# One fused attention-and-experts kernel: other places for its last batch's shared work, for four list scatters and for a semaphore's first count

## The reference

```python
def ffn(x, gate_w, w1, w2, w3, ws1, ws2, ws3):
    scores = softmax(xf @ gate_w.T)
    weights, idx = top_k(scores, 2)                  # 2 of 8 experts per token
    h = einsum('td,eid->eti', xf, w1)
    g = silu(h) * einsum('td,eid->eti', xf, w3)
    eo = einsum('eti,edi->etd', g, w2)
    y = einsum('etd,te->td', eo, comb)               # comb: the two weights
    z = silu(xf @ ws1.T) * (xf @ ws3.T) @ ws2.T      # the shared expert
    return y + z
x = x + tanh(g_xattn) * cross_attention(layernorm(x), ctx)
x = x + tanh(g_ffn) * ffn(layernorm(x))
```

## Time and profile before

| what | us |
|---|---|
| median of 3 runs (lowest, highest) | 464.53 (464.41, 466.38) |
| the profiled execution, its own time | 467.39 |
| its span in the trace | 465.7 |
| TensorE busy | 409.3 (88%) |
| VectorE busy | 306.2 (66%) |
| ScalarE busy | 239.5 (51%) |
| GpSimd busy | 228.1 (49%) |

### The profile page before, as it was taken

The page is one execution under the profiler, slowest core; times in us unless marked ns, Lnnn a source line. Parts: engine busy times, 40 slices in busy tenths (PEclk is TensorE's granted clock), DMA queues, the critical chain, the costliest instruction groups (busy, mean ns, idle before and its releaser), DMA issues.

```text
span 465.7 us, 8278 instructions
## 1 busy us (share of the span) xinstructions
PE 409.3 (88%) x2739; PEld 221.6 (48%) x2740; DVE 306.2 (66%) x663; ACT 239.5 (51%) x432; POOL 228.1 (49%) x205
## 2 busy tenths in 40 slices
PE   1877887999999999898868889989999999999980
PEld 1454443555545554464433345445555555555540
DVE  4977998789588876898839659954444444444430
ACT  2786875676647766756214136834443434344330
POOL 4008434537266762589350212755556565565422
PEclk9988998999999999999979899999999999999996
DMA  8930002606006076176168477966567666566553
GB/s 303 419 104 2 0 1 68 227 2 223 4 1 227 2 288 134 41 262 192 59 59 155 138 272 225 158 116 109 118 98 131 128 100 130 94 132 108 96 67 45
DMA packets 20768, 58.64 MB, mean 126 GB/s; under 512 B 3521, under 2 KB 3777, under 8 KB 20354
## 3 DMA queue, kind: packets, MB, share of 16 engines
q1 hardware_dynamic: 11234, 37.77, 25.9%
q0 software_dynamic: 9504, 20.48, 24.5%
HBM read 35.54 MB, written 22.70 MB: 125 GB/s over the span
## 4 chain that ended last, share of the span: by engine, by line
PE 54%; DVE 17%; POOL 8%; issue 8%; DMA 5%; ACT 5%; POOLq 1%; SPq 0%; DVEq 0%; ACTq 0%
PE bank L1664 40%; PE bank L1669 9%; DVE arena L1057 4%; ACT arena L701 3%; DMA lists<-pair,slot 2%; DVE mv L1093 2%; POOL lists L573 2%; POOL arena L588 2%; PE bank L1817 2%; PE bank L1806 2%; PE bank L1794 2%; POOL GT L613 2%; DVE mx L1178 1%; POOL ln L555 1%; DMA listed<-lists 1%
## 5 line engine op out<-in xcount | busy, mean ns | idle before, releaser
L1664 PE MATMUL bank<-arena,GT 128*128 x468 | 107.4, 379 | 2.8 <-issue 2.8
L685 POOL DMA_INDIRECT out<-rows,entry x39 | 61.8, 1586 | 72.1 <-issue 31.3
L1664 PE MATMUL bank<-arena,gT 128*128 (+1 forms) x336 | 80.2, 376 | 1.4 <-ACT rows L1032 1.0
L1664 PEld LDWEIGHTS bank<-arena,GT 128*128 128x128 f16 x468 | 45.8, 98 | 49.7 <-issue 3.5
L701 ACT ACTIVATE arena<-bank 128x512 f16<-128x512 f32 (+1 forms) x88 | 48.7, 587 | 26.1 <-PE bank L1664 12.0
L662 POOL DMA_INDIRECT rows<-xrows,entry x39 | 38.9, 997 | 43.4 <-DVE entry L1455 18.2
L1057 DVE SCALAR_TENSOR_TENSOR arena<-bank,arena 128x512 f16<-128x512 f32 (+1 forms) x72 | 44.7, 667 | 11.5 <-ACT arena L701 9.0
L1664 PEld LDWEIGHTS bank<-arena,gT 128*128 128x128 f16 x336 | 32.7, 98 | 37.6 <-issue 2.5
L1664 PE MATMUL bank<-arena,x2T 128*128 128x512 f16 x192 | 47.7, 400 | 2.1 <-DVE x2T L1056 1.7
L1056 DVE TENSOR_TENSOR gT<-bank,gT 128x256 f16<-128x256 f32 x55 | 23.0, 420 | 38.8 <-ACT gT L701 38.7
L1623 DVE SCALAR_TENSOR_TENSOR uu<-th,bank 128x256 f32<-128x256 f32 x39 | 16.4, 421 | 48.5 <-ACT th L999 46.8
(11 more groups left out here) (174 smaller groups left out, 648.3 us busy)
## 6 DMA issues: line engine op xcount, KB each, us to landing
x_sb<-in_experts SPq DMA_DIRECT2D x9, 768.0 KB, 4.7
rows<-in_experts SPq DMA_DIRECT2D x6, 768.0 KB, 6.2
xrows<-xn SPq DMA_DIRECT2D x16, 256.0 KB, 6.2
out<-x_sb SPq DMA_DIRECT2D x16, 256.0 KB
image<-GT SPq DMA_DIRECT2D x5, 768.0 KB, 4.2
arena<-image SPq DMA_DIRECT2D x10, 384.0 KB
x_sb<-in_x SPq DMA_DIRECT2D x1, 2048.0 KB, 15.5
x_sb<-in_x SPq DMA_DIRECT2D x2, 512.0 KB, 4.2
```

The lines of the kernel that those rows point to most:

```text
L685: nc.gpsimd.indirect_dma_start(out=out, out_offset=bass.IndirectOffsetOnAxis(ap=entry[:, 1, j:j + 1], axis=0), in_=Y[:, j % RING, :], in_o ...
L1664: last = nc.tensor.matmul(dst, a, b, start=n == 0, stop=n == len(steps) - 1)
```

## The change

Nothing is computed otherwise and no instruction is added but waits; what moves is the place of work on each engine.

- GpSimd: the second four scatters of batch 2 wait for `lg_out` of batch 3.
- SP: the first count of `landed` stands ahead of the image loads; the load of `listed` stands ahead of piece 11's, and piece 12 is loaded ahead of the last stores of batch 2.
- VectorE: the two first `turn_lo` of batch 3's x2 move up into `last_attention`; in `last_feed_forward` the bases 8 and 9 (batch 2, tiles 0 and 1) come sooner, two halves (14, 15) are split there, and steps 0 to 4 of the second part split halves 16 to 30, step 5 only 31. `base(3, 3)` comes behind `hidden_e(0)`.
- TensorE: two turns of g ahead of the second logits, `hidden(3, 3)` and `down(2, 3)` ahead of `place_lists`, and `down(3, 3)` behind `hidden_e(0)`.

```diff
@@ -361,9 +361,9 @@
 
         PIECES = 2 * E
         PARTS = 4
-        HI_AT_TURN = {1: (20, 21), 2: (22, 23), 3: (24, 25), 4: (27, 28), 5: (30, 31)}
-        HI_AT_END = {3: (26,), 4: (29,)}
-        LO_FIRST = 7
+        HI_AT_TURN = {1: (20, 21), 2: (22, 23), 3: (25, 26), 4: (28, 29), 5: (31,)}
+        HI_AT_END = {2: (24,), 3: (27,), 4: (30,)}
+        LO_FIRST = 8
         LO_STEPS = 6
         FIRST_ROUNDS = -(-E // RING)
         ROUTE2 = 7
@@ -449,6 +449,7 @@
                     sp.wait_ge(w_split[w_slot(k)], PARTS * (w_round(k) - 1))
                 sp.dma_start(w_raw(k), raw_of(k)).then_inc(ld_w[w_slot(k)], 16)
 
+            sp.sem_inc(landed, 1)
             sp.wait_ge(st_init, 32)
             load_image_raw(0)
             sp.wait_ge(shared_lo, 2)
@@ -484,23 +485,21 @@
             store_rows(B - 1, 2, PER)
             sp.wait_ge(st_base, 16 * (PER * (B - 2) + 1))
             load_piece(9)
-            sp.wait_ge(st_rows, 16 * NT)
-            sp.wait_ge(turned, turn_no(B, "x2", PER - 1)[0])
-            load_piece(11)
             for n in range(2):
                 sp.wait_ge(st_pairs[n], 16 * 2 * PER * (B // 2 - n))
             sp.dma_start(listed[:, :, :].rearrange("p r c -> p (r c)"),
                          lists[:, :].rearrange("(p f) c -> p (f c)", p=P)).then_inc(ld_listed, 16)
+            sp.wait_ge(st_rows, 16 * NT)
+            sp.wait_ge(turned, turn_no(B, "x2", PER - 1)[0])
+            load_piece(11)
+            sp.wait_ge(h_mm, NT)
+            load_piece(12)
             store_base(B - 2, 1, PER)
             sp.wait_ge(st_base, 16 * PER * (B - 1))
             load_piece(10)
-            sp.wait_ge(h_mm, NT)
-            load_piece(12)
             store_base(B - 1)
             for k in range(13, PIECES):
                 load_piece(k)
-            sp.sem_inc(landed, 1)
-
 
             for j in range(TILES):
                 sp.wait_ge(added[j % RING], 16 * (j // RING + 1))
@@ -646,7 +645,9 @@
                 scatter_pairs(prev - 1, (1,))
                 power2(b, 0)
                 power2(b, 1)
-                scatter_pairs(prev)
+                scatter_pairs(prev, (0,))
+                pool.wait_ge(lg_out, B)
+                scatter_pairs(prev, (1,))
 
             power1(1)
             softmax_mask(0)
@@ -808,6 +809,8 @@
                     for v in range(2):
                         nc.scalar.activation(send[:, 1 + v, g, :], in_row[:, g, :], ACT.Copy,
                                              scale=sent[:, v, g:g + 1]).then_inc(sends, 1)
+
+            def got0_high():
                 act.wait_ge(ld_listed, 16)
                 hi(got0[:, 1, :], listed[:, :, 1].bitcast(F32), S_SEND).then_inc(got0_hi, 1)
 
@@ -880,17 +883,16 @@
                 tanh_h(f, 0)
                 turn_hi(c, "x2", 2)
                 turn_hi(c, "x2", 3)
+                turn_hi(f, "g", 2)
+                turn_hi(f, "g", 3)
                 router_exp(f)
                 tanh_h(f, 1)
-                turn_hi(f, "g", 2)
-                turn_hi(f, "g", 3)
+                tanh_h(f, 2)
                 send_lists()
-                tanh_h(f, 2)
-                turn_hi(c, "g", 0)
-                turn_hi(c, "g", 1)
                 tanh_h(f, 3)
-                turn_hi(c, "g", 2)
-                turn_hi(c, "g", 3)
+                got0_high()
+                for i in range(PER):
+                    turn_hi(c, "g", i)
                 split_piece(9)
 
             def probabilities_hi(b, i):
@@ -1350,7 +1352,9 @@
                 norm2(b, 0)
                 x1_and_statistics(b, 2)
                 x1_and_statistics(b, 3)
+                turn_lo(b + 1, "x2", 0)
                 aggregate2(b, 1)
+                turn_lo(b + 1, "x2", 1)
                 router_place(f)
 
             def both(v):
@@ -1478,22 +1482,21 @@
             def last_feed_forward(f):
 
                 c = f + 1
-                turn_lo(c, "x2", 0)
-                turn_lo(c, "x2", 1)
                 norm2(f, 1)
+                base(f - 1, 0)
                 hidden(f, 0)
                 turn_lo(c, "x2", 2)
                 turn_lo(c, "x2", 3)
-                base(f - 1, 0)
+                turn_lo(f, "g", 2)
+                turn_lo(f, "g", 3)
                 router_logits(f)
                 router_choose(f, 0)
                 router_choose(f, 1)
                 sent_weights()
                 last_place(f)
-                turn_lo(f, "g", 2)
-                turn_lo(f, "g", 3)
+                hidden(f, 1)
+                base(f - 1, 1)
                 rows_hot()
-                hidden(f, 1)
                 blocks_hot()
                 pick_tiles()
                 listed_before()
@@ -1501,17 +1504,18 @@
                 turn_lo(c, "g", 0)
                 read_entries()
                 read_table()
-                base(f - 1, 1)
                 base(f - 1, 2)
+                hidden(f, 2)
                 turn_lo(c, "g", 1)
-                hidden(f, 2)
                 read_weights()
+                split_half(2 * LO_FIRST - 2)
+                split_half(2 * LO_FIRST - 1)
                 base(f - 1, 3)
+                turn_lo(c, "g", 2)
                 hidden(f, 3)
                 base(f, 0)
-                turn_lo(c, "g", 2)
+                turn_lo(c, "g", 3)
                 base(f, 1)
-                turn_lo(c, "g", 3)
                 base(f, 2)
 
             def shared_lo_half(h):
@@ -1637,14 +1641,14 @@
                     split_half(2 * LO_FIRST + 3 * j)
                 if nxt:
                     hidden_e(j + 1, (s + 1) % RING)
-                if isinstance(j, int) and j < LO_STEPS:
+                if isinstance(j, int) and j < LO_STEPS - 1:
                     for n in (1, 2):
                         split_half(2 * LO_FIRST + 3 * j + n)
 
             rows_lo(0, 0)
-            base(B - 1, 3)
             rows_lo(1, 1)
             hidden_e(0, 0)
+            base(B - 1, 3)
             for it in range(FIRST_ROUNDS):
                 for s in range(RING):
                     step(it, s)
@@ -1895,23 +1899,23 @@
                 turn_x2(f, 2)
                 turn_x2(f, 3)
                 router(0, 2)
+                turn_g(f - 1, 2)
+                turn_g(f - 1, 3)
                 down(f - 1, 1)
                 split_done(c, "x2", 3)
                 router(2, 4).then_inc(lg_mm, 1)
                 hidden(f, 1)
-                turn_g(f - 1, 2)
-                turn_g(f - 1, 3)
                 count_pairs(f)
                 hidden(f, 2)
                 down(f - 1, 2)
+                hidden(f, 3)
+                down(f - 1, 3)
                 place_lists()
                 turn_g(f, 0)
                 find_entries()
                 turn_g(f, 1)
-                hidden(f, 3)
-                down(f - 1, 3)
+                down(f, 0)
                 turn_g(f, 2)
-                down(f, 0)
                 down(f, 1)
                 turn_g(f, 3)
                 down(f, 2)
@@ -2040,11 +2044,11 @@
 
             pe.wait_ge(weight_ready, 2)
             pe.wait_ge(table_ready, 2)
+            e = expert_of(0)
             turn_rows(0, 0, 0)
+            turn_rows(1, 1, 0)
+            hidden_e(0, 0, e)
             down(B - 1, 3)
-            turn_rows(1, 1, 0)
-            e = expert_of(0)
-            hidden_e(0, 0, e)
             pe.wait_ge(base_ready, NT)
             for it in range(FIRST_ROUNDS):
                 for s in range(RING):
```

## The result

The changed kernel takes 462.85 us (median of 12 runs, 459.05 to 467.67), the kernel before in the same rounds 466.73 (12 runs, 464.28 to 469.08). The ratio is 0.9902 with a 95% interval of 0.9874 to 0.9930: faster by about 1%, 4.6 us of the kernel before. The medians lie only 3.9 us apart, as the ratio leaves out two executions of the changed kernel in a slower state. The forecast ratio was 459.8 / 464.53 = 0.9899. The size came out; the working behind it only in part.

The account below looks back on a forecast made before the run. TensorE held 54% of the chain, so other work bound the kernel too, at the lists. Savings of 3.0 (steps), 1.4 (find) and 0.3 (find to `hidden_e(1)`) sum to 4.7 us: median 464.53 to 459.8, range 455.5 to 463.7.

Parts of the forecast that it names:

- The steps: Second part, `hidden_e(1)` to `hidden_e(7)`: six steps without rests take 27.2 us against 30.2, saving 3.0 us.
- F to `hidden_e(1)`: Stretch from the find to `hidden_e(1)`, paced by VectorE: 18.2 us against 18.5, saving 0.3 us.
- F: Time of the find, behind scatters and list load: 257.1 against 258.5, saving 1.4 us; between 254.2 and 261.2.
- rival (a): Batch 3's second logits are still slowed, losing the same 4.8 us: 461.7 us in total; chance 0.18.
- Gathers and adds: Second part: gather 5 at F + 25.8, hidden with 1.1 us to spare; first tiles' adds don't wait for loads.
- The sum: Whole kernel: savings of 3.0 + 1.4 + 0.3 = 4.7 us, giving a median of 459.8 us.
- (b): TensorE's clock stays at half from around the find to `hidden_e(0)`: 463.5 us, little change; chance 0.15.
- (c): Faster case: the scatters drain in 5.6 us and the clock holds, F = 254.2: 456.9 us; chance 0.12.
- (d): Slower case: the new wait turns slow logits into late lists, `lg_out` 10.8 us late: 470.6 us; chance 0.10.
- The rule weighed: DMA during the scatters: stalled writes stall other queues too, so the logits would be caught as before; speaks against the change.

Follow-up runs that it names:

- e2: The changed kernel with the old split order of the weight halves in the second part, splits and SP's count as before; 0.9965 of before.
- e11: The changed kernel with SP's first count of `landed` back behind its loads; 0.9885 of before.
- e6: The changed kernel with batch 3's shared work, `hidden(3, 3)` and `down(2, 3)`, back behind the find; 0.9938 of before.
- e1: The changed kernel measured again, unaltered, as yardstick; 464.26 us, 0.9959 of before.
- e7: The changed kernel with piece 7's two halves split where VectorE rests and TensorE's wait for all bases moved ahead of step 0's down product; 458.46 us, 0.9785 of before.
- e3: The changed kernel without GpSimd's wait of the second four scatters for the last logits; 1.0027 of before.
- e10: The changed kernel without GpSimd's wait for the last logits, measured again in another group; 1.0005 of before.
- e12: The kernel before with only the wait of the second four scatters for the last logits added; 1.0019 of before.
- e4: The changed kernel with piece 9's load moved behind the list load; 0.9942 of before.
- e8: The kernel of e7 with piece 9's load moved behind the list load as well; 0.9805 of before.
- e9: The changed kernel measured a third time, unaltered, as yardstick; 0.9879 of before.
- e5: The changed kernel with batch 2's eight scatters left out, so its list entries are missing; one run, 458.24 us.

## Why the prediction came out, point by point

- **The steps, 3.0 us forecast.** Measured 30.20 - 27.24 = 2.96, with no rest, and by e2 and e11 it is the halves and not SP's count that did it. Right, but it was counted as pure gain.
- **F to `hidden_e(1)`, forecast F + 18.2 and 0.3 saved.** Measured 18.78, 0.3 lost. The walk held piece by piece: the second down product at F + 5.6 (`down(3, 1)`, forecast 6.4), the second turn of rows at F + 12.3 (12.5), `hidden_e(0)` done at F + 15.5 (15.3), the last base at F + 17.6 (17.4); 0.5 of issue behind that base was missing. What the sum of this stretch hid is that it holds a gain of 2.1 (e6) and a cost of 3.2 (e2), and that the cost belongs to the edit booked with 3.0. (Both hold a share of half clock; without it they are about 1.2 and 1.8.) Net, the split's move gained nothing that e1 and e2 could show, and by e7's rows most of its cost could be had back.
- **F, forecast 257.1 or 1.4 us saved: the step that failed.** Measured from the anchor, F came 0.4 sooner (0.7 in e1). The scatters were sized well: last one at 39.5 (forecast 38.7 from the anchor), list load issued at 46.7 (47.2), 7.2 behind it (8.5, the middle between 11.3 and a lower end of 5.6 that is 0.4 more than its own sum of 3.9 and 1.27). The load landed in 2.1, sooner than my 3.9. By the lists alone F would have been near 50. What failed is the sentence on the logits: "This is no term of its own, since the lists' chain was last". The logits came 4.3 sooner as forecast, VectorE then lost 4.5 us in rests between mask and slots, and this chain, slots, ScalarE's 16 one-hots, find, became the last. I had the rests as something of the logits' place (rival (a)); e3, e10 and e12 show them at whatever stands at that time.
- **Gathers and adds.** Right: TensorE never waits for gather 5, which comes at F + 20.7, sooner than my F + 25.8, and the first add follows 2.3 behind its rows.
- **The sum.** Forecast 3.0 + 1.4 + 0.3 = 4.7; in the profiled pair 2.96 + 0.41 - 0.28 + 0.15 (behind `hidden_e(7)`) = 3.2 us. The timed gain of 4.6 lies above it, e1's (0.4%, 1.9 us) below: the middle of the three comparisons is the forecast, but the terms bear 3.2 rather than 4.7, and that it hit so closely is partly luck.
- **The rivals.** (a) in part: something is still slowed, only behind the logits. (b): half clock came at 262 to 266 (0.57) and costs 1.4, but the kernel before had about as much of it in 260 to 264 (0.59), so by this estimate it gave no difference. (c) did not occur: its F would be 49.5 from the anchor, and none with scatters reached it; e7 came nearest with 50.8, by the short load, while the scatters drained no faster (18 to 20 us in all). (d) did not occur: `lg_out` came 4.3 sooner, not later.
- **The rule weighed.** I had named the Trainium skill (DMA: Bandwidth & Descriptors, "Back-pressure in remote DMA"), by which stalled writes stall the other queues too. In e4 DMA is 2% busy, and scatters and rests are nearly as in after, so here it decides nothing; whether it is at work in the earlier trace rows no run shows. Its section "Anatomy of one DMA" gives a transfer from GpSimd some 2.0 us of fixed cost: eight one behind another would be 16, an estimate from that page. The runs show 18.1 to 20.3 from the first issue to the list load, and landings 2.0 apart on average in e6 to e8, so they behave nearly as if they went one by one.

**What stays open.** What the rests are. They show as idle time of 0.5 to 4.7 us that no recorded wait explains, on TensorE, VectorE or ScalarE, between the first scatter's issue and the list load; e3, e10 and e12 show that they keep to that time and not to an instruction. They stand between mask and slots in the profiles of after, e1, e2, e4, e9 and e12, and ahead of the mask in those of before, e3 and e10; e11, with e9's instructions up to there, has only those ahead of the logits (slots at 40.8 and not 45.4); e5 to e8 have none. That the scatters cause them is argued from place and time only, and beside the sixteen scatters of the batches before, issued in fours, VectorE has in every profile but the same waits for ScalarE (0.8 and 1.6 us), rests or no rests later. Two rivals:

- *The engines wait for their own instructions to be loaded.* The trace records these transfers. In after one of them (8 KB) falls between mask and slots, beside four rests; in e7 two fall there, and there is no rest. This speaks against it without settling it.
- *The recording of the trace has a part in them.* The eight scatters make 128 completions. The traces of e6, e7 and e8, without rests, hold all 128; those with rests hold 49 (after), 53 (e1), 69 (e2), 49 (e4), 56 (e9), 89 (before), 90 (e12), 100 (e10), 103 (e3) and 107 (e11). So rests and missing records go together here. Which brings which isn't shown, nor how often executions without a trace have rests; that the wait for the logits pays in 12 executions of e3 and of e1 each says that something of them is real.

## What to carry to other kernels

An engine's earlier start on later work is paid where its queue is short: look for what the instructions now stand ahead of, and put them in a stretch in which that engine rests, as e7 did with the same instructions (1.7 of its 3.2 us). Where two chains join (here lists and logits at the find), shortening the last gains only up to the other, and a chain that was hidden must be walked with its own rests. Work moved into an engine's rest lengthens the path of whatever must pass behind it: with the logits late, the 18 matmuls moved ahead of the lists set the find (e3). Before a pair of profiles is read, subtract them at a point ahead of which no work was moved: here 2.4 of 5.6 us were not the change's.

## What the hardware showed that I had not expected

- Eight indirect scatters of 128 entries of 8 bytes take 18 to 20 us from the first issue until the list load may go, with DMA 2% busy in e4 as well as 84 to 104% before, with a gap of 2.8 us among them or none: about 2.4 us each. Where all completions are recorded (e6 to e8), the first lands 5.3 to 5.6 us behind its issue and the others 2.0 apart on average.
- A plain load of 128 KB landed in 2.1 us with nothing in flight ahead of it (after; DMA 0% busy in the microsecond before) and in 5.1 with two loads of weights in flight (before).
- The same kernel's stretch at half clock fell ahead of the find in one execution (e9, 1.9 us) and behind it in two others (after and e1, 1.4 us).
